# A state-space layer with an FP4 feed-forward block on one core: the transposes of x move behind those of h and into the layer's PSUM bank

## The chip, the cores and the metric

The kernel runs on one core of a Trainium2 chip. The metric is the device time of one launch in microseconds (us). A NeuronCore has five engines that run side by side, each with its own queue in program order: TensorE (PE in the profile; PEld is its weight load), VectorE (DVE), ScalarE (ACT), GpSimd (POOL) and SyncE (SP), which here issues the DMAs. They wait for one another through semaphores.

## The reference, cut to what matters

Only the first sizes differ from the helper code: x is 4 x 2048 x 256, the feed-forward width is 704, the state has 16 entries.

```python
def L0_attn(x, A, B, C, D, gamma, beta):
    xB = jnp.einsum('bsh,nh->bsn', x, B)
    xD = jnp.einsum('bsh,oh->bso', x, D)
    def step(state, xb_t):
        state = state @ A.T + xb_t
        return (state, state)
    _, states = jax.lax.scan(step, init, jnp.swapaxes(xB, 0, 1))
    out = jnp.einsum('bsn,hn->bsh', states, C) + xD
    return layernorm(out) * gamma + beta

def fp4_quant_dequant(x):                  # blocks of 16 along the last dim
    scale = max(max(abs(xb)) / 6.0, 1e-12)
    idx = jnp.searchsorted(_MID, jnp.abs(xb / scale))
    return _GRID[idx] * sign(xb) * scale

def L0_ffn(x, w_gate, w_up, w_down):       # each product quantises both operands
    gate = fp4_linear(x, w_gate)
    y = fp4_linear(x, w_up)
    return fp4_linear(jax.nn.silu(gate) * y, w_down)

x = layernorm(x + L0_attn(x, ...))
x = layernorm(x + L0_ffn(x, ...))
```

## The kernel before

A first phase of about 70 us loads x and the weights, quantises and transposes the weights and computes the chunk states of the scan. After it a pipeline runs over 64 tiles of 128 rows. Each tile passes through these operations:

- **layer** (PE, L1017 and the helper's L1006): C times the states plus D times x, into the PSUM bank `yb`, columns 0 to 255. Then `mean_square` (ACT L573), the reciprocal root on POOL (L457), `scale_gamma` (DVE L760, which works in `yb` itself) and `add_x` (DVE L767, the last reader of `yb`, semaphore `s_x1p`). ACT's `norm2` (L647) gives x1.
- Quantisation of x1: `x_max`, `x_scale` and `x_recip` on DVE, `x_norm` on POOL (L467), `x_abs` on ACT, `x_sum` (L788) and `x_grid` (L794) on DVE, and last `x_scale` on POOL (L472, semaphore `s_qx`).
- **x_turn** (PE L1027): two transposes of the quantised x1 into `xt`, which is part of the PSUM tensor `turned`. `x_hi` (ACT L610) copies them to `xtHi`, `x_lo` (DVE L799, semaphore `s_xlo`) computes the rest into `xtLo`.
- **gu0, gu1, gu2** (PE L1006): the gate and up products in three column cuts, six products each, into the three banks of `gu`. `silu_gate` (ACT L614) and `times_up` (DVE L806, which waits for the end of gu2) follow.
- Quantisation of h: `h_max`, `h_scale` and `h_recip` on DVE (L810, L815, L820), `h_norm` on POOL (L477), `h_abs` on ACT, `h_sum` (L825) and `h_grid` (L830) on DVE, `h_scale` on POOL (L482, semaphore `s_qh`).
- **h_turn** (PE L1059): six transposes into `ht`, which shares its bank of `turned` with `xt`. `h_hi` (ACT L627) and `h_lo` (DVE L835, `s_lo`) follow.
- **ffn_down** (PE L1006, 18 products into `db`), `add_x1` (DVE L842, `s_r`), and the last layernorm on ACT and POOL; SP stores the tile.

The order on each engine is written out by hand: a list of operations, each with a lag. In step s, an operation with lag k works on tile s - k. The lists are unrolled in program order, so each engine runs one tile of every operation in each step:

```python
run(pe, [(h_turn, 6), (gu1, 4), (gu2, 4), (x_turn, 3), (layer, 0), (ffn_down, 6), (gu0, 3)], ...)
run(pool, [(h_norm, 6), (x_scale, 4), (pow3, 10), (t_lo, 0), (add_beta, 0), (x_norm, 3), (pow2, 2),
           (h_scale, 6), (pow1, 1)])
run(dve, [(x_grid, 2), (scale_gamma, 0), (x_max, 1), (add_x, 0), (x_scale, 1), (h_lo, 5), (x_recip, 1),
          (h_sum, 4), (times_up, 3), (h_grid, 4), (x_lo, 2), (h_max, 3), (add_x1, 5), (h_scale, 3),
          (x_sum, 1), (h_recip, 3)], ...)
```

Below, n is the tile whose h PE turns in a step. In that step PE works on h_turn(n), gu1 and gu2(n+2), x_turn(n+3), layer(n+6), ffn_down(n) and gu0(n+3). From the lists follows what lies side by side on the others: DVE runs `h_lo(n)`, `h_sum(n+1)`, `times_up(n+2)`, `h_grid(n+1)`, `x_lo(n+3)`, `h_max(n+2)`, `add_x1(n)`; POOL runs `h_norm(n+1)` and right behind it `x_scale(n+3)`.

Of the kernel before, what the change touches and what calls it, by code (L numbers as in the profile page):

```python
# [48 lines left out]
def ssm_fp4_ffn(nc, x, A, B, C, D, gamma, beta, w_gate, w_up, w_down, out):  # L49
    BATCH, SEQ, H = x.shape  # L50
# [4 lines left out]
    TILES = HALVES * CHUNK  # L55
# [46 lines left out]
    with ExitStack() as ctx:  # L102
# [3 lines left out]
        def bank(name):  # L106
            return ctx.enter_context(nc.psum_tensor(name, [P, 512], F32))
# [84 lines left out]
        yb = bank("yb")  # L192
        turned = ctx.enter_context(nc.psum_tensor("turned", [P, 2 * 512], F32))
# [1 line left out]

        GU_CUTS = [(0, 512), (512, 1024), (1024, GU)]
        amH = gu[:, GU:GU + FB]
        xt = turned[:, 0:H]
        ht = turned[:, H:H + NKD * P]
        db = turned[:, 512:512 + H]  # L200
        hm = grid[:, 0:FF]
# [59 lines left out]
        def run(eng, ops, after={}):  # L261


            last = max(lag for _, lag in ops)

            def step(h, i, inside):
                for op, lag in ops:
                    if inside or 0 <= CHUNK * h + i - lag < TILES:
                        op(h, i - lag)

            for h in range(PEELED):
                for i in range(CHUNK):
                    step(h, i, False)
                    for extra in after.get(CHUNK * h + i, ()):
                        extra()
            with eng.Fori(PEELED, HALVES) as h:
                for i in range(CHUNK):
                    step(h, i, True)
            for i in range(last):
                step(HALVES, i, False)  # L280

        def done(h, m):

            return h * CHUNK + (m + 1)

        def done_dma(h, m):

            return h * (16 * CHUNK // RING) + 16 * (m // RING + 1)

        def w_target(g, low):  # L290

            _, what, k, n = W_GROUPS[g]
            src = wbanks[g % 3]
            if what == "gu":
                dst = (wguLo if low else wguHi)[:, :, k * P:(k + n) * P].rearrange("p c (r k) -> p r c k", k=P)
                return dst, src[:, 0:n * KH * P].rearrange("p (r c k) -> p r c k", r=n, c=KH)
            first = 0 if what == "dA" else KDA
            return ((wdLo if low else wdHi)[:, first:first + KDA, k * P:(k + 1) * P],
                    src[:, 0:KDA * P].rearrange("p (c k) -> p c k", k=P))
# [554 lines left out]
        def _(pe):  # L854
# [77 lines left out]
            def chunk_states(b, positions=range(CHUNK)):  # L932

                pe.wait_ge(s_gc, KH)
                pe.wait_ge(s_xtc, 4 * KH * (b + 1))
                for t in positions:
                    for c in range(KH):
                        ins = nc.tensor.matmul(fBank[b // BPP][:, b % BPP * CPB:(b % BPP + 1) * CPB],  # L938
                                               gPad[:, c, N * t:N * t + P], xT[:, t, c, b * CPB:(b + 1) * CPB],
                                               start=(b % BPP == 0 and t == 0 and c == 0),  # L940
                                               stop=(t == CHUNK - 1 and c == KH - 1), skip_group_check=True)
                if CHUNK - 1 in positions:
                    ins.then_inc(s_loc, 1)
# [58 lines left out]
            def split_products(to, terms, first=True):  # L1002

                passes = [(l, r) for (lh, ll), (rh, rl) in terms for l, r in ((lh, rh), (lh, rl), (ll, rh))]
                for q, (l, r) in enumerate(passes):
                    ins = nc.tensor.matmul(to, l, r, start=(first and q == 0), stop=(q == len(passes) - 1))  # L1006
                return ins

            def layer(h, m):

                r = m % RING
                tile = h * CHUNK + m
                pe.wait_ge(s_tlo, done(h, m))
                pe.wait_ge(s_ld[r], 3 * done_dma(h, m))
                if not isinstance(tile, int) or tile >= 1:
                    pe.wait_ge(s_x1p, done(h, m - 1))
                nc.tensor.matmul(yb[:, 0:H], stTile[:, r, :], cStack[:, :], start=True, stop=False)  # L1017
                split_products(yb[:, 0:H], [((tHi[:, m % 2, c, :], tLo[:, m % 2, c, :]), (dHi[:, c, :], dLo[:, c, :]))
                                            for c in range(KH)], first=False).then_inc(s_y, 1)

            def x_turn(h, m):
                tile = h * CHUNK + m
                pe.wait_ge(s_qx, done(h, m))
                if not isinstance(tile, int) or tile >= 3:
                    pe.wait_ge(s_lo, done(h, m - 3))
                for c in range(KH):
                    ins = nc.tensor.transpose(xt[:, c * P:(c + 1) * P], xm[:, m % 2, c * P:(c + 1) * P], ident[:, :])  # L1027
                ins.then_inc(s_tx, 1)

            def ffn_up(k):  # L1030
                first, last = GU_CUTS[k]

                def op(h, m):
                    tile = h * CHUNK + m
                    if k == 0:
                        pe.wait_ge(s_xlo, done(h, m))
                    if not isinstance(tile, int) or tile >= 1:
                        pe.wait_ge([s_silu, s_h, s_hsc][k], done(h, m - 1))
                    ins = split_products(gu[:, first:last],
                                         [((xtHi[:, m % 2, c, :], xtLo[:, m % 2, c, :]),  # L1040
                                           (wguHi[:, c, first:last], wguLo[:, c, first:last])) for c in range(KH)])
                    if k >= 1:
                        ins.then_inc([s_gate, s_up][k - 1], 1)
                return op

            def h_turn(h, m):
                tile = h * CHUNK + m
                pe.wait_ge(s_qh, done(h, m))
                if not isinstance(tile, int) or tile >= 1:
                    pe.wait_ge(s_lo, done(h, m - 1))  # L1050
                    pe.wait_ge(s_r, done(h, m - 1))
                else:
                    pe.wait_ge(s_states, PAIRS)
                if isinstance(tile, int) and tile + 2 >= TILES:
                    pe.wait_ge(s_xlo, TILES)
                else:
                    pe.wait_ge(s_xlo, done(h, m + 2))
                for q, row in enumerate(KD):
                    ins = nc.tensor.transpose(ht[:, q * P:(q + 1) * P], hq[:, m % 2, row:row + P], ident[:, :])  # L1059
                ins.then_inc(s_t, 1)  # L1060

            def ffn_down(h, m):
                tile = h * CHUNK + m
                pe.wait_ge(s_lo, done(h, m))
                if isinstance(tile, int) and tile == 0:
# [3 lines left out]

            chunk_states(BATCH - 1, FILL_STATES[-1])  # L1070
            gu0, gu1, gu2 = (ffn_up(k) for k in range(3))
            run(pe, [(h_turn, 6), (gu1, 4), (gu2, 4), (x_turn, 3), (layer, 0), (ffn_down, 6), (gu0, 3)],
                {step_: [*(lambda ts=ts: chunk_states(BATCH - 1, ts) for ts in (FILL_STATES.get(step_),) if ts),
                         *(lambda k=k: link(1, k) for k in FILL_CHAIN.get(step_, ()))] for step_ in range(CHUNK)})

# [27 lines left out]
```

## Time and profile before

| what | value |
|---|---|
| time, median of 3 runs | 636.41 us (634.6 to 637.58) |
| the profiled execution: time | 634.62 us |
| its span | 632.8 us |
| PE busy | 602.9 us (95%) |
| DVE, ACT, POOL busy | 514.5, 477.8, 465.6 us |
| TensorE clock granted, mean | 0.973 of full speed |

The span is the stretch from the first to the last recorded instruction; the time of a run holds 1.8 us more. The busy time of an engine is what its instructions cover. Matmuls overlap one another in the records, so the pace of PE is read from the distance of their starts rather than from their durations.

### The profile page before, as it was taken

The numbers are of one execution on the slowest core, as the hardware profiler recorded it, in microseconds if no ns is written. First come the engines' busy times: TensorE is split into PE (matmuls) and PEld (weight loads), VectorE is DVE, ScalarE is ACT, GpSimd is POOL, SyncE is SP. The second block draws the span as 40 slices with busy tenths as digits, with TensorE's granted clock in tenths as the row PEclk, the third lists the DMA queues.
The fourth block names the chain that finished last, engine by engine and source line by source line (L and its number), as shares of the span: only waits on it lengthen the run. The fifth ranks groups of instructions, "written<-read, shape, count | busy, mean of one in ns | idle before, by whom it ended". The sixth has DMA issues, their size and how long they took to land.

```text
span 632.8 us, 12672 instructions
## 1 busy us (share of the span) xinstructions
PE 602.9 (95%) x3705; PEld 525.8 (83%) x3705; DVE 514.5 (81%) x1226; ACT 477.8 (75%) x1422; POOL 465.6 (74%) x602
## 2 busy tenths in 40 slices
PE   5999968999999999999999999999999999999984
PEld 3787747788888888888888888888888888888874
DVE  2694126999999999999999999999999999999972
ACT  3455326778888888888888888888888888888764
POOL 1461316878888888888888888888888888887652
PEclk9999957999999999999999999999999999999996
DMA  6743111111111111111111111111111111110001
GB/s 247 260 138 101 46 30 50 42 38 46 53 54 54 53 47 54 52 46 53 53 53 53 53 53 53 52 50 48 53 52 52 53 52 45 53 34 9 25 18 41
DMA packets 46171, 38.32 MB, mean 61 GB/s; under 512 B 6912, under 2 KB 44864, under 8 KB 45120
## 3 DMA queue, kind: packets, MB, share of 16 engines
q1 hardware_dynamic: 46144, 37.99, 19.5%
q8 instruction: 13, 0.21, 0.1%
q14 instruction: 14, 0.11, 0.1%
HBM read 19.50 MB, written 8.39 MB: 44 GB/s over the span
## 4 chain that ended last, share of the span: by engine, by line
PE 90%; ACT 3%; DVE 2%; issue 1%; DMA 1%; POOL 1%; SPq 1%; POOLq 0%; DVEq 0%; ACTq 0%
PE gu L1006 39%; PE turned L1006 21%; PE yb L1006 9%; PE turned L1059 7%; PE yb L1017 3%; PE turned L1027 2%; PE gu L938 2%; PE yb L912 2%; PE gu L912 1%; DMA scratch<-in_L_attn_x_dram 1%; PE turned L938 1%; ACT xT L525 1%; PE turned L974 1%; SPq L377 1%; POOL scratch L482 0%
## 5 line engine op out<-in xcount | busy, mean ns | idle before, releaser
L1006 PE MATMUL gu<-wguHi,xtHi 128*128 128x512 f32 (+1 forms) x384 | 151.0, 393 | 1.3 <-DVE xtLo L799 1.3
L1006 PE MATMUL gu<-wguLo,xtHi 128*128 128x512 f32 (+1 forms) x384 | 145.6, 379 | 0.0
L1006 PE MATMUL gu<-wguHi,xtLo 128*128 128x512 f32 (+1 forms) x384 | 145.5, 379 | 0.0
L477 POOL TENSOR_TENSOR scratch<-scratch 128x704 f32<-128x704 f32 x64 | 92.3, 1442 | 57.5 <-DVE scratch L820 57.5
L1006 PE MATMUL turned<-wdHi,htHi 128*128 128x256 f32 x384 | 109.9, 286 | 3.8 <-DVE htLo L835 3.8
L1006 PE MATMUL turned<-wdLo,htHi 128*128 128x256 f32 x384 | 109.2, 284 | 0.0
L1006 PE MATMUL turned<-wdHi,htLo 128*128 128x256 f32 x384 | 108.4, 282 | 0.0
L482 POOL TENSOR_TENSOR scratch<-scratch 128x704 f32<-128x704 f32 x64 | 89.1, 1392 | 9.5 <-DVE scratch L830 9.4
L627 ACT CAST htHi<-turned 128x768 fp32r<-128x768 f32 x64 | 51.4, 804 | 57.9 <-PE turned L1059 57.9
L1006 PEld LDWEIGHTS gu<-wguHi,xtHi 128*128 128x128 f32 x384 | 73.0, 190 | 11.4 <-DVE xtLo L799 2.1
L1006 PEld LDWEIGHTS gu<-wguHi,xtLo 128*128 128x128 f32 x384 | 72.6, 189 | 11.7
L1006 PEld LDWEIGHTS gu<-wguLo,xtHi 128*128 128x128 f32 x384 | 72.8, 189 | 9.1
L1006 PEld LDWEIGHTS turned<-wdHi,htHi 128*128 128x128 f32 x384 | 72.6, 189 | 4.2 <-DVE htLo L835 4.2
L1006 PEld LDWEIGHTS turned<-wdHi,htLo 128*128 128x128 f32 x384 | 73.8, 192 | 0.0
L1006 PEld LDWEIGHTS turned<-wdLo,htHi 128*128 128x128 f32 x384 | 73.0, 190 | 0.0
L835 DVE TENSOR_TENSOR htLo<-turned,htHi 128x768 fp32r<-128x768 f32 x64 | 61.3, 958 | 13.3 <-ACT htHi L627 6.2
L842 DVE SCALAR_TENSOR_TENSOR scratch<-turned,scratch 128x256 f32<-128x256 f32 x64 | 27.2, 424 | 42.5 <-PE turned L1006 42.5
L462 POOL TENSOR_TENSOR tLo<-xtTile,tHi 128x256 fp32r<-128x256 f32 x64 | 47.4, 740 | 18.2 <-ACT tHi L606 18.2
L806 DVE TENSOR_TENSOR scratch<-scratch,gu 128x704 f32<-128x704 f32 x64 | 56.0, 875 | 2.3 <-PE gu L1006 2.3
L810 DVE TENSOR_REDUCE gu<-scratch 128x44 f32<-128x704 f32 x64 | 56.6, 884 | 0.0
L830 DVE SCALAR_TENSOR_TENSOR scratch<-grid,scratch 128x704 f32<-128x704 f32 x64 | 56.6, 884 | 0.0
L1059 PEld LDWEIGHTS turned<-ident,scratch 128*128 128x128 f32 x384 | 45.7, 140 | 10.9 <-POOL scratch L482 2.4
(169 smaller groups left out, 1593.4 us busy)
## 6 DMA issues: line engine op xcount, KB each, us to landing
scratch<-in_L_attn_x_dram SPq DMA_DIRECT2D x8, 1024.0 KB, 5.1
xtTile<-xT SPq DMA_DIRECT2D x64, 128.0 KB, 2.3
scratch<-in_L_attn_x_dram SPq DMA_DIRECT2D x64, 128.0 KB, 2.4
out_dram<-scratch SPq DMA_DIRECT2D x64, 128.0 KB, 1.9
stTile<-statesHi SPq DMA_DIRECT2D x128, 8.0 KB, 1.7
stTile<-statesLo SPq DMA_DIRECT2D x64, 8.0 KB, 1.7
scratch<-in_L_ffn_w_down_dram SPq DMA_DIRECT2D x1, 704.0 KB, 7.5
scratch<-in_L_ffn_w_up_dram SPq DMA_DIRECT2D x1, 640.0 KB, 6.0
```

Of the source, the lines that this page charges most:

```text
L462: nc.gpsimd.tensor_tensor(tLo[:, m % 2, :, :], xtTile[:, m % RING, :, :], as_f32(tHi[:, m % 2, :, :]), ALU.subtract).then_inc(s_tlo, 1)
L477: nc.gpsimd.tensor_tensor(blocks(hx[:, m % 2, :]), blocks(hx[:, m % 2, :]), each_block(hRc[:, m % 4, :], FB), ALU.mult).then_inc(s_xnh, 1)
L482: nc.gpsimd.tensor_tensor(blocks(hq[:, m % 2, :]), blocks(hq[:, m % 2, :]), each_block(hSc[:, m % 4, :], FB), ALU.mult).then_inc(s_qh, 1)
L627: nc.scalar.copy(htHi[:, m % 2, :, :].rearrange("p c k -> p (c k)"), ht).then_inc(s_hi, 1)
L806: nc.vector.tensor_tensor(hx[:, m % 2, :], silu[:, m % 2, :], gu[:, FF:GU], ALU.mult).then_inc(s_h, 1)
L810: nc.vector.tensor_reduce(amH, blocks(hx[:, m % 2, :]), AX_X, ALU.max, apply_absolute_value=True).then_inc(s_ham, 1)
L830: nc.vector.scalar_tensor_tensor(out=hq[:, m % 2, :], in0=hm, scalar=LEAST, in1=hx[:, m % 2, :], op0=ALU.max, op1=ALU.subtract, reverse1=T ...
L835: nc.vector.tensor_tensor(htLo[:, m % 2, :, :].rearrange("p c k -> p (c k)"), ht, as_f32(htHi[:, m % 2, :, :]).rearrange("p c k -> p (c k) ...
L842: nc.vector.scalar_tensor_tensor(out=x1[:, j, :], in0=db, scalar=1.0, in1=x1[:, j, :], op0=ALU.mult, op1=ALU.add, accum_out=sum3[:, j:j + ...
L912: ins = nc.tensor.transpose(to[:, q * P:(q + 1) * P], xRaw[:, h % 2, (t * KH + q) * P:(t * KH + q + 1) * P], ident[:, :])
L1006: ins = nc.tensor.matmul(to, l, r, start=(first and q == 0), stop=(q == len(passes) - 1))
L1059: ins = nc.tensor.transpose(ht[:, q * P:(q + 1) * P], hq[:, m % 2, row:row + P], ident[:, :])
```

## The change

`xt`, the target of x's two transposes, leaves the bank of `turned` that it shared with `ht` and becomes columns 256 to 511 of the layer's bank `yb`. In PE's list x_turn moves from behind gu2 to right behind h_turn. The waits are changed to fit: x_turn no longer waits for `h_lo` of three tiles back but for `add_x` of tile m+2 (`s_x1p`), which ends the use of `yb` by the layer's result; h_turn no longer waits for `x_lo`; and layer(m) now waits for `x_lo(m-3)`, the last reader of `xt`.

```diff
-        xt = turned[:, 0:H]
+        xt = yb[:, H:2 * H]
@@ layer
                     pe.wait_ge(s_x1p, done(h, m - 1))
+                if not isinstance(tile, int) or tile >= 3:
+                    pe.wait_ge(s_xlo, done(h, m - 3))
                 nc.tensor.matmul(yb[:, 0:H], stTile[:, r, :], cStack[:, :], start=True, stop=False)
@@ x_turn
                 pe.wait_ge(s_qx, done(h, m))
-                if not isinstance(tile, int) or tile >= 3:
-                    pe.wait_ge(s_lo, done(h, m - 3))
+                if isinstance(tile, int) and tile + 2 >= TILES:
+                    pe.wait_ge(s_x1p, TILES)
+                else:
+                    pe.wait_ge(s_x1p, done(h, m + 2))
@@ h_turn
-                if isinstance(tile, int) and tile + 2 >= TILES:
-                    pe.wait_ge(s_xlo, TILES)
-                else:
-                    pe.wait_ge(s_xlo, done(h, m + 2))
@@ the order on PE
-            run(pe, [(h_turn, 6), (gu1, 4), (gu2, 4), (x_turn, 3), (layer, 0), (ffn_down, 6), (gu0, 3)],
+            run(pe, [(h_turn, 6), (x_turn, 3), (gu1, 4), (gu2, 4), (layer, 0), (ffn_down, 6), (gu0, 3)],
```

On PE, at the head of a step (h_turn, L1059), before the change:

```order
 L1059 MATMUL turned<-ident,scratch 128x128 [waits s_r,s_xlo,s_lo,s_qh]
 L1059 MATMUL turned<-ident,scratch 128x128 x5
 L1006 MATMUL gu<-wguHi,xtHi 128x512 [waits s_h]
 L1006 MATMUL gu<-wguLo,xtHi 128x512
 L1006 MATMUL gu<-wguHi,xtLo 128x512
```

And in the changed kernel, the same place:

```order
 L1059 MATMUL turned<-ident,scratch 128x128 [waits s_r,s_lo,s_qh]
 L1059 MATMUL turned<-ident,scratch 128x128 x5
 L1031 MATMUL yb<-ident,scratch 128x128 [waits s_x1p,s_qx]
 L1031 MATMUL yb<-ident,scratch 128x128
 L1006 MATMUL gu<-wguHi,xtHi 128x512 [waits s_h]
 L1006 MATMUL gu<-wguLo,xtHi 128x512
```

The two transposes of x, with their wait for POOL's `s_qx`, now stand ahead of the twelve products of gu1 and gu2.

On PE, between the end of gu2 and ffn_down, before the change:

```order
 L1006 MATMUL gu<-wguHi,xtLo 128x384
 L1027 MATMUL turned<-ident,scratch 128x128 [waits s_lo,s_qx]
 L1027 MATMUL turned<-ident,scratch 128x128
 L1017 MATMUL yb<-cStack,stTile 128x256 [waits s_x1p,s_ld2,s_tlo]
 L1006 MATMUL yb<-dHi,tHi 128x256
```

And in the changed kernel:

```order
 L1006 MATMUL gu<-wguLo,xtHi 128x384
 L1006 MATMUL gu<-wguHi,xtLo 128x384
 L1019 MATMUL yb<-cStack,stTile 128x256 [waits s_x1p,s_xlo,s_ld2,s_tlo]
 L1006 MATMUL yb<-dHi,tHi 128x256
 L1006 MATMUL yb<-dLo,tHi 128x256
```

The layer now follows gu2 directly and has one more wait, for DVE's `s_xlo`. On DVE the order is the same before and after; around the instruction that signals `s_xlo` (L799) the changed kernel has:

```order
 L825 SCALAR_TENSOR_TENSOR scratch<-grid,scratch 128x704 [waits s_mh]
 L806 TENSOR_TENSOR scratch<-scratch,gu 128x704 [waits s_up,s_silu]
 L830 SCALAR_TENSOR_TENSOR scratch<-grid,scratch 128x704 [waits s_hsum]
 L799 TENSOR_TENSOR xtLo<-yb,xtHi 128x256 [waits s_xhi]
 L810 TENSOR_REDUCE gu<-scratch 128x44 [waits s_h]
```

Nothing moved there; what L799 reads is now `yb`. It stands behind `times_up` (L806), whose `s_up` is signalled by the last product of gu2.

## Rows read from the trace of the kernel before

**Rows 1.** The page, its first two parts: busy time, and PE and clock in 40 slices.
```profile
PE 602.9 (95%) x3705; PEld 525.8 (83%) x3705; DVE 514.5 (81%) x1226; ACT 477.8 (75%) x1422; POOL 465.6 (74%) x602
...
PE   5999968999999999999999999999999999999984
...
PEclk9999957999999999999999999999999999999996
```

**Rows 2.** Timeline of PE, one step: start us, duration, engine, line, operands, count.
```profile
301.86 0.82 PE L1059 MATMUL turned<-ident,scratch 128*128 128x128 f32 x6
...
302.43 0.48 PE L1006 MATMUL gu<-wguHi,xtHi 128*128 128x512 f32 x1
...
304.81 0.34 PE L1006 MATMUL gu<-wguHi,xtLo 128*128 128x384 f32 x1
...
304.98 0.38 PE L1027 MATMUL turned<-ident,scratch 128*128 128x128 f32 x2
...
305.29 0.38 PE L1017 MATMUL yb<-cStack,stTile 48*128 48x256 f32 x1
...
306.42 0.28 PE L1006 MATMUL turned<-wdHi,htHi 128*128 128x256 f32 x1
...
308.46 0.28 PE L1006 MATMUL turned<-wdHi,htLo 128*128 128x256 f32 x1
```

**Rows 3.** The same timeline, DVE and POOL, with idle time before and its releaser.
```profile
300.65 0.42 DVE L842 SCALAR_TENSOR_TENSOR scratch<-turned,scratch 128x256 f32<-128x256 f32 x1 [0.65 <-PE turned L1006]
...
301.45 0.42 DVE L820 RECIPROCAL scratch<-scratch 128x44 f32<-128x44 f32 x1
...
301.95 1.44 POOL L477 TENSOR_TENSOR scratch<-scratch 128x704 f32<-128x704 f32 x1 [0.95 <-DVE scratch L820]
...
303.36 0.62 POOL L472 TENSOR_TENSOR scratch<-scratch,xSc 128x256 f32<-128x256 f32 x1
...
305.33 0.88 DVE L806 TENSOR_TENSOR scratch<-scratch,gu 128x704 f32<-128x704 f32 x1
...
306.92 0.42 DVE L799 TENSOR_TENSOR xtLo<-turned,xtHi 128x256 fp32r<-128x256 f32 x1
...
308.78 0.43 DVE L842 SCALAR_TENSOR_TENSOR scratch<-turned,scratch 128x256 f32<-128x256 f32 x1 [0.65 <-PE turned L1006]
```

**Rows 4.** Timeline, late: x_turn ahead of ffn_down, and PE released by DVE.
```profile
603.59 0.38 PE L1027 MATMUL turned<-ident,scratch 128*128 128x128 f32 x2
603.72 0.36 PE L1006 MATMUL turned<-wdHi,htHi 128*128 128x256 f32 x1
...
615.91 0.96 DVE L835 TENSOR_TENSOR htLo<-turned,htHi 128x768 fp32r<-128x768 f32 x1 [1.55 <-ACT htHi L627]
...
616.93 0.39 PE L1006 MATMUL turned<-wdHi,htHi 128*128 128x256 f32 x1 [1.88 <-DVE htLo L835]
```

**Rows 5.** Timeline, early: DVE released by the end of gu2.
```profile
104.85 0.34 PE L1006 MATMUL gu<-wguHi,xtLo 128*128 128x384 f32 x1
...
105.29 0.89 DVE L806 TENSOR_TENSOR scratch<-scratch,gu 128x704 f32<-128x704 f32 x1 [2.27 <-PE gu L1006]
```

**Rows 6.** PE by stretches: us, PE busy (instructions), granted clock, DMA share, GB/s.
```profile
75.00:80.00 5.00, 4.08 (x26) 0.94 0.31 85
80.00:85.00 5.00, 2.90 (x16) 0.50 0.27 73
...
620.00:622.00 2.00, 0.87 (x6) 1.00 0.00 0
622.00:624.00 2.00, 1.13 (x5) 0.54 0.18 65
```

**Rows 7.** Timeline of PE at the low clock, and where it rose again.
```profile
97.43 0.58 PE L1017 MATMUL yb<-cStack,stTile 48*128 48x256 f32 x1
...
99.38 0.63 PE L1006 MATMUL gu<-wguHi,xtHi 128*128 128x512 f32 x1
...
103.51 0.40 PE L1006 MATMUL gu<-wguLo,xtHi 128*128 128x512 f32 x1
```

## The prediction, made before the changed kernel was run

> **What bounds the kernel now.** I read the page first: PE is busy 95% of the span, the others 74 to 81%, and PE's digits are 9 from the eighth slice to the third from the end, at full clock [rows 1]. The next view is the timeline of one step. Two `add_x1` (DVE L842) stand at 300.65 and 308.78 us, so a step lasts 8.13 us [rows 3]; the first slices and the last ones are start and end, and between them one step repeats. PE's rows of that step show no gap: h_turn at 301.86, gu1 at 302.43, the end of gu2 at 304.81 + 0.34 = 305.15, x_turn at 304.98, the layer at 305.29, ffn_down from 306.42 to 308.46 + 0.28 = 308.74 [rows 2]. DVE waits 0.65 us for ffn_down in every step and POOL 0.95 us for DVE's `h_recip` [rows 3]. So PE sets the pace and the other engines follow it with about a microsecond in hand.
>
> With so full an engine the question for a moved instruction is not what it costs, but whether its operands are there at the new place. The new order puts two waits on PE that the trace lets one date.
>
> **The first wait: x_turn on POOL.** In this step x_turn(n+3) needs POOL's `x_scale(n+3)` (L472), which ends at 303.36 + 0.62 = 303.98 [rows 3]. At its old place, 304.98, that was done a microsecond before. At the new place PE arrives at 302.43 [rows 2], 1.6 us too early. POOL cannot be earlier: x_scale stands right behind `h_norm(n+1)` (L477, from 301.95), which waits for `h_recip(n+1)` (DVE L820, 301.45 + 0.42), which stands behind `add_x1(n-1)` (300.65), which waits for the end of the previous step's ffn_down [rows 3]. So this is no fixed delay that slides away once the engines are shifted; it ties x_turn to PE's own previous ffn_down. Behind the waiting x_turn everything of PE is queued: gu1, gu2, the layer, ffn_down. The other new wait there, `add_x(n+5)`, ends earlier in the same DVE pass than `h_lo`, well before POOL is done, and costs nothing.
>
> **The second wait: the layer on x_lo.** layer(n+6) now waits for `x_lo(n+3)` of the same step. DVE runs it behind `times_up(n+2)` and `h_grid(n+1)`, and times_up waits for the end of gu2(n+2), which PE has only just finished. From the start of times_up at 305.33 to the end of x_lo at 306.92 + 0.42 = 307.34 are 2.01 us [rows 3]. Before, the layer started at 305.29, two microseconds ahead of that end [rows 2]; nothing asked it to wait. This wait follows gu2 wherever gu2 is, so it comes on top of the first. Behind it are queued the layer, ffn_down, gu0 and h_turn.
>
> **The ring and its length.** Both waits lie on one closed ring, which I add up from the end of one ffn_down to the end of the next:
> - ffn_down ends 308.74, add_x1 starts 308.78, 0.04 later; from add_x1 to the start of h_norm 301.95 - 300.65 = 1.30 [rows 2, 3]. Sum 1.34.
> - h_norm start to x_scale end: 303.98 - 301.95 = 2.03 [rows 3].
> - PE takes up work after a wait 616.93 - 616.87 = 0.06 later [rows 4].
> - x_turn takes 603.72 - 603.59 = 0.13 where nothing holds the next product [rows 4]; gu1 start to gu2 end 305.15 - 302.43 = 2.72 [rows 2]. Sum 2.85.
> - gu2 end to times_up: 105.29 - 105.19 = 0.10 where DVE waited for it [rows 5].
> - times_up start to x_lo end 2.01, and 0.06 until PE starts [rows 3, 4].
> - layer start to the end of ffn_down 308.74 - 305.29 = 3.45 [rows 2].
>
> The sum is 1.34 + 2.03 + 0.06 + 2.85 + 0.10 + 2.01 + 0.06 + 3.45 = 11.90 us against 8.13, so 3.77 us more for each step. What the step holds beside (gu0, h_turn, h_hi, h_lo, silu, the layernorms, the loads) runs in the gaps of this ring: h_turn is over 302.43 - 300.61 = 1.8 us after the end of the previous ffn_down (308.74 - 8.13 = 300.61), and x_turn starts 3.4 us after it. The work taken away saves nothing here: the wait ahead of the old layer (0.31 from x_turn to the layer instead of 0.13) lay on PE, but the ring contains a fresh wait in its place.
>
> **How many steps.** ffn_down runs for tiles 0 to 57 while the layer still runs, which makes 57 whole rings: 57 x 3.77 = 214.9 us. In steps 3 to 6, the start, ffn_down does not close the ring; the layer's wait costs at least 0.10 + 2.01 + 0.06 = 2.17 and at most 3.77 each. I take 2.4, near the lower end, since h_norm does not yet hold POOL in the first of them: 9.6. In the last three steps with an x_turn there is no layer, and only the first wait is paid, at most 304.04 - 302.43 = 1.61 each; I take 4 for the three. Together 228.5. The profiled execution has a span of 632.8, so 861.3, and with the 1.8 us that lie outside the span 863.1. The median of the runs is 1.8 above the profiled time, so **865** if the clock holds. Errors of 0.1 us a ring would make 6 us.
>
> **The clock.** PE then works 8 of 12 us, with gaps of 1.6 and 2.2 us in each ring. The trace shows the granted clock fall from full to half speed (2.4 to 1.2 GHz) in two places. Between 75 and 80 PE was busy 4.08 of 5 us, with small products, and the clock was 0.50 from 80 on; around 622 it fell behind a stretch with 0.87 busy of 2 us [rows 6]. At the low level the layer took 99.38 - 97.43 = 1.95 us instead of 1.13, and the products were back at 0.40 us each from 103.51, about 6 us after PE had begun to work without a gap [rows 7]. In the ring the stretch without a gap (layer, ffn_down, gu0) lasts 4.8 us at full clock. So a fall in a gap costs between nothing (clock holds) and half of 6 us = 3.0 for each ring. The ring resembles the two places where it fell in that PE waits again and again for an answer from another engine; its runs between the waits are denser than there. I take the middle of the two prices, 1.5 us a ring: 61 x 1.5 = 91.5, and 865 + 91.5 = **956**.
>
> The Trainium skill (TensorE: Matmul & The Clock Gate, section "Why this matters for your kernels") ties a drop in the middle of a kernel to idle gaps longer than either of the two here; by it the clock holds and the time is the 865. The trace does not quite agree with that: at 75 to 80 us the clock fell though PE was idle for less than 1 of 5 us [rows 6].
>
> **The rivals.**
> - *The clock holds* (865). For it: in the tail, at 620 to 622, it was still full with PE busy under half of the time [rows 6]. Against it: the fall right behind that.
> - *It stays low for the whole dense run, or falls in both gaps* (956 to 865 + 61 x 3.0 = 1048). For it: the rise took 6 us in the start.
> - *Only the first wait counts*, because x_lo is done before the layer gets there. Then the ring is 1.34 + 2.03 + 0.06 + 0.13 + (304.98 - 302.43) + 3.45 = 9.56, 1.43 more; 57 x 1.43 and some 10 for the ends give 728. Against it: DVE's order puts x_lo behind times_up without exception.
> - *Only the second wait counts*: 61 x 2.17 = 132, 769. It would need POOL's x_scale to run ahead of h_norm; its list says otherwise.
> - *Faster*: the transposes stand together, and the layer is no longer held behind its own: 0.31 - 0.13 = 0.18 for each of 61 steps, 11 us, 625. It decides at one point: `x_scale(n+3)` would have to end before 302.43, and it ends at 303.98; and x_lo before 305.15, and it ends at 307.34. Both are behind work that needs PE's previous result.
>
> **How the numbers follow.** Clock falls once a ring 0.58 (its own range 925 to 1005), clock holds 0.26, longer low stretches beyond 1005 0.08, one wait alone 0.05, faster 0.02, within the noise 0.01. The predicted time is that of the likeliest case, 956. The range reaches from 855, to take in the case of a held clock with its error, to 1005; outside are the upper end of the clock's price and the single waits. A measurement of this kernel can tell about 0.5% from no change, and nearly all cases are slower by far more.
>
> **What would show it.** In the profile after: the distance of two add_x1 11.9 us with a full clock, up to 13.5 with a fall; PE idle ahead of x_turn by 1.6 us, put down to POOL L472, some 60 times; PE idle ahead of the layer by 2.2 us, put down to DVE L799 (xtLo), 61 times; DVE's times_up waiting for gu2, which it hardly did before; PE's clock row with digits of 6 to 9 instead of 9. If PE has no gap ahead of the layer, my reading of the lags is wrong; if the distance is 11.9 and the clock row still reads 9, the sum was right and the clock's term was not.

## The result, and the profile after

| | before | after |
|---|---|---|
| time, median | 635.62 us (4 runs) | 948.47 us (4 runs, 946.23 to 950.09) |
| ratio | | 1.491 (95% interval 1.487 to 1.495) |
| span of the profiled execution | 632.8 us | 948.3 us |
| PE busy | 602.9 us (95%) | 698.6 us (74%) |
| mean granted clock of TensorE | 0.973 | 0.877 |

The changed kernel takes half as long again. The forecast was 956, in a range of 855 to 1005. The page of the changed kernel, the lines that answer to [rows 1]:

```profile
PE 698.6 (74%) x3705; PEld 601.0 (63%) x3705; DVE 520.3 (55%) x1226; ACT 475.6 (50%) x1422; POOL 469.4 (49%) x602
...
PE   6997677767776686767777677766777677767785
...
PEclk8987888898988989888898988989889898888996
```

DVE, ACT and POOL have the same work as before and less of the span; PE has the same 3705 matmuls, but 96 us more of busy time, and in the repeating part its clock row reads 8 and 9 by turns where it read 9 before. The view of the waits (who waited for whom, total us, times, longest us) names both new waits, the one for x_lo 61 times and the one for POOL 62 times:

```profile
DVE scratch L842 <- PE turned L1006: 244.6, 60, 4.3
...
PE yb L1019 <- DVE xtLo L799: 136.5, 61, 2.3
...
PE yb L1031 <- POOL scratch L472: 82.9, 62, 2.4
```

The first line is the mirror image: DVE, which waited 0.65 us a step for ffn_down [rows 3], now waits 2.8 or 4.3 us, because everything of PE comes later. One step of the timeline, in order of time (it answers to [rows 2, 3]; L1019 is the layer's first product, L1031 x_turn, both shifted by the new lines):

```profile
501.08 0.89 DVE L806 TENSOR_TENSOR scratch<-scratch,gu 128x704 f32<-128x704 f32 x1 [1.61 <-PE gu L1006]
...
502.69 0.41 DVE L799 TENSOR_TENSOR xtLo<-yb,xtHi 128x256 fp32r<-128x256 f32 x1
...
503.25 0.35 PE L1019 MATMUL yb<-cStack,stTile 48*128 48x256 f32 x1 [2.27 <-DVE xtLo L799]
...
503.53 0.52 PE L1006 MATMUL yb<-dHi,tHi 128*128 128x256 f32 x1
...
504.92 0.41 PE L1006 MATMUL turned<-wdHi,htHi 128*128 128x256 f32 x1
...
507.05 0.28 PE L1006 MATMUL turned<-wdLo,htHi 128*128 128x256 f32 x1
...
508.19 0.42 DVE L842 SCALAR_TENSOR_TENSOR scratch<-turned,scratch 128x256 f32<-128x256 f32 x1 [4.29 <-PE turned L1006]
...
509.40 0.82 PE L1059 MATMUL turned<-ident,scratch 128*128 128x128 f32 x6
...
509.49 1.44 POOL L477 TENSOR_TENSOR scratch<-scratch 128x704 f32<-128x704 f32 x1 [2.75 <-DVE scratch L820]
...
510.89 0.62 POOL L472 TENSOR_TENSOR scratch<-scratch,xSc 128x256 f32<-128x256 f32 x1
...
511.56 0.44 PE L1031 MATMUL yb<-ident,scratch 128*128 128x128 f32 x2 [1.35 <-POOL scratch L472]
...
514.55 0.89 DVE L806 TENSOR_TENSOR scratch<-scratch,gu 128x704 f32<-128x704 f32 x1 [1.61 <-PE gu L1006]
```

Read from top to bottom this is the ring of the prediction: the end of gu2 releases times_up, x_lo follows behind h_grid, x_lo releases the layer, ffn_down's end releases add_x1, then h_recip, h_norm, x_scale, and x_scale releases x_turn. From one times_up to the next are 13.47 us. The layer's products in this step take 504.92 - 503.25 = 1.67 us instead of the 1.13 of [rows 2], and those of ffn_down are recorded at 0.41 us each instead of 0.28, until 0.28 returns at 507.05: the clock is at its lower level there. The windows view of PE around this step (columns: length, busy, clock, DMA share, GB/s):

```profile
500.00:503.00 3.00, 0.97 (x6) 1.00 0.00 0
503.00:507.00 4.00, 3.75 (x17) 0.58 0.00 0
507.00:511.00 4.00, 3.22 (x22) 1.00 0.23 71
```

The clock falls just behind the gap ahead of the layer, not in it, and is full again before ffn_down ends. In the repeating part its record turns to one half 0.1 to 1.8 us behind the start of the layer, a little later from one fall to the next, and after the latest ones comes a step without a fall. Of the 57 distances between the add_x1 of tiles 0 to 57, six are 11.98 to 12.00 us and 51 are 13.15 to 13.53, most of them 13.48: a step without and a step with a fall. Their mean is 13.29.

### The profile page after: what moved, and what is told of

It is laid out like the page before. It is cut to its first block, busy times and chain, and to the rows that moved or that the text cites. A ratio compares the mean times of both kernels' runs of the same rounds, so it can differ in the third digit from the quotient of the medians.

```text
span 948.3 us, 12661 instructions
## 1 busy us (share of the span) xinstructions
PE 698.6 (74%) x3705; PEld 601.0 (63%) x3705; DVE 520.3 (55%) x1226; ACT 475.6 (50%) x1422; POOL 469.4 (49%) x602
## 4 chain that ended last, share of the span: by engine, by line
PE 54%; DVE 21%; issue 12%; POOL 9%; ACT 2%; DMA 1%; SPq 0%; POOLq 0%; DVEq 0%; ACTq 0%
PE turned L1006 19%; PE gu L1006 17%; PE yb L1006 7%; DVE scratch L806 6%; DVE scratch L830 5%; POOL scratch L472 4%; POOL scratch L477 4%; PE yb L1031 3%; DVE scratch L842 2%; PE yb L1019 2%; DVE xtLo L799 2%; DVE scratch L820 2%; DVE scratch L788 2%; PE gu L938 2%; PE yb L912 1%
## 5 line engine op out<-in xcount | busy, mean ns | idle before, releaser
L1006 PE MATMUL turned<-wdHi,htHi 128*128 128x256 f32 x384 | 141.1, 367 | 3.8 <-DVE htLo L835 3.8
L1006 PE MATMUL turned<-wdLo,htHi 128*128 128x256 f32 x384 | 140.1, 365 | 0.0
L1006 PE MATMUL turned<-wdHi,htLo 128*128 128x256 f32 x384 | 139.2, 362 | 0.0
L1019 PE MATMUL yb<-cStack,stTile 48*128 48x256 f32 x64 | 23.2, 362 | 140.1 <-DVE xtLo L799 136.5
L1019 PEld LDWEIGHTS yb<-cStack,stTile 48*128 48x128 f32 x64 | 11.9, 187 | 158.5 <-issue 158.5
L806 DVE TENSOR_TENSOR scratch<-scratch,gu 128x704 f32<-128x704 f32 x64 | 56.8, 888 | 100.7 <-PE gu L1006 100.7
L1006 PEld LDWEIGHTS turned<-wdHi,htHi 128*128 128x128 f32 x384 | 107.3, 279 | 4.3 <-DVE htLo L835 4.3
L1006 PEld LDWEIGHTS turned<-wdLo,htHi 128*128 128x128 f32 x384 | 107.0, 279 | 0.0
L1006 PEld LDWEIGHTS turned<-wdHi,htLo 128*128 128x128 f32 x384 | 106.2, 277 | 0.0
L614 ACT ACTIVATE scratch<-gu 128x704 f32<-128x704 f32 x64 | 48.6, 760 | 105.0 <-PE gu L1006 105.0
L1031 PE MATMUL yb<-ident,scratch 128*128 128x128 f32 x128 | 28.2, 302 | 87.4 <-POOL scratch L472 82.9
L457 POOL TENSOR_TENSOR rs<-ve1t,neg_half 128x1 f32<-128x1 f32 x64 | 35.4, 553 | 98.3 <-ACT ve1t L580 98.3
L457 POOL TENSOR_TENSOR rs<-ve2t,neg_half 128x1 f32<-128x1 f32 x64 | 35.2, 549 | 96.0 <-ACT ve2t L580 96.0
```

Source lines behind the costliest of these rows:

```text
L457: nc.gpsimd.tensor_tensor(dst[:, j:j + 1], src[:, j:j + 1], neg_half[:, :], ALU.pow).then_inc(signal, 1)
L614: nc.scalar.activation(silu[:, m % 2, :], gu[:, 0:FF], ACT.Silu).then_inc(s_silu, 1)
L806: nc.vector.tensor_tensor(hx[:, m % 2, :], silu[:, m % 2, :], gu[:, FF:GU], ALU.mult).then_inc(s_h, 1)
```

## The experiments

The theory has three terms: the wait of x_turn for POOL, the wait of the layer for x_lo, and a fall of the clock in the gap that the second one leaves. The first four kernels take one of them away each (in e3 a wait for h_lo stands in for the one for POOL).

**e1, work added.** If the clock's term is real, giving PE something to do in the gap must make the kernel faster. Edit, in `layer`, ahead of its waits for add_x and x_lo:

```diff
+                if not isinstance(tile, int) or tile >= 6:
+                    pe.wait_ge(s_lo, done(h, m - 6))
+                    for _ in range(12):
+                        nc.tensor.matmul(db, wdHi[:, 0, 0:P], wdHi[:, 1, :], start=True, stop=True)
```

> The changed kernel plus twelve extra products of 256 columns on PE between gu2 and the layer's new wait, from constant weights into the bank that ffn_down overwrites; they wait for h_lo of the tile, as ffn_down does. They add about 12 x 0.12 = 1.4 us of work a step and lie wholly in the 2.2 us gap ahead of the layer. Theory (the ring of two waits sets 11.9 us a step, and a fall of the clock in that gap adds 1.6): the ring is as long as before, the clock does not fall, the step is 11.9 us and the time about 863, some 85 us below the changed kernel although PE does more. Rival 1 (the step of 13.5 is the ring's own length, the clock is a by-product): the fillers change nothing, 948. Rival 2 (PE's own work is what counts): 1.4 us a step more, about 1035.

Measured 874.51 us, 1.375 of before (1.370 to 1.380), 74 us less than the changed kernel. With 58 x 12 products more the kernel is faster. Its clock row and the step's rows (timeline; L1018 is the filler, L1023 the layer):

```profile
PEclk9999589999999999999999999999999999999998
```

```profile
502.22 1.60 PE L1018 MATMUL turned<-wdHi 128*128 128x256 f32 x12
...
502.49 0.89 DVE L806 TENSOR_TENSOR scratch<-scratch,gu 128x704 f32<-128x704 f32 x1 [1.62 <-PE gu L1006]
...
504.09 0.41 DVE L799 TENSOR_TENSOR xtLo<-yb,xtHi 128x256 fp32r<-128x256 f32 x1
...
504.65 0.36 PE L1023 MATMUL yb<-cStack,stTile 48*128 48x256 f32 x1 [0.84 <-DVE xtLo L799]
```

The fillers lie in the wait and shorten PE's idle time from 2.27 to 0.84 us, the clock stays full between the start and the end, and all 57 steps read 11.98 to 12.04 us. The six steps without a fall in the changed kernel read the same. So the ring is 11.99 us long and the clock cost 13.29 - 11.99 = 1.30 us a step on the mean, 1.49 in a step with a fall. The time is 11.5 us above the expected 863; where they lie is said below, under the ends. Rival 1 (948) and rival 2 (1035) fall.

**e2, the bank alone.** The changed kernel with `run(pe, ...)` in the old order, x_turn behind gu2.

> The changed kernel with PE's old order: x_turn stands behind gu2 again, its target stays in the layer's bank with both new waits. Theory: the first wait (POOL's x_scale) goes, the second (layer on x_lo) stays, since DVE's x_lo is behind times_up either way: 8.13 + 2.0 = 10.2 us a step with a full clock, 757 us, and up to 1.6 us a step more (855) where the clock falls in that gap; I expect something between, near 800. Rival (the move on PE is what costs, the bank is harmless): near 636.

Measured 780.6 us (one run). Its steps are 10.28 us, with a pair of about 11.4 and 12.1 every nine or ten steps where the clock fell, ten steps of the 57 in all, 10.55 on the mean. The wait for POOL is gone and the one for x_lo stands as before:

```profile
PE yb L1019 <- DVE xtLo L799: 127.8, 61, 2.7
```

The bank's wait costs 10.28 - 8.13 = 2.15 us a step with x_turn at its old, harmless place. The rival (near 636) falls.

**e3, the order alone.** The kernel before with x_turn moved in PE's list and nothing else, so that x's target stays in `turned`.

> The kernel before with only PE's order changed: x_turn directly behind h_turn, its target still in h's bank, so that it waits for h_lo of the h just turned instead of add_x, and the layer has no new wait. Theory: x_turn waits both for x_scale (3.4 us after ffn_down's end) and for h_lo (about 3.9 us after it), the wait ahead of the layer is absent: 3.95 + 2.68 + 3.45 = 10.1 us a step with a full clock, 745 us, up to 1.6 us a step more (835) where the clock falls in the gap of 2.1 us. Rival (x_turn's place is harmless, only the bank's wait costs): near 636.

Measured 773.65 us (one run), steps of 10.26 us. PE waits for h_lo here, as the old bank demands, and not ahead of the layer:

```profile
504.35 0.41 PE L1027 MATMUL turned<-ident,scratch 128*128 128x128 f32 x2 [1.97 <-DVE htLo L835]
```

The move alone costs 2.13 us a step, nearly what the bank alone costs, and no step of the repeating part has a fall. The bank change was the way to avoid this wait for h_lo, but POOL's x_scale is nearly as late: it ends at 503.67 here, 0.53 us before h_lo. The wait for POOL itself is not measured by this kernel but by the next one.

**e4, x_lo early.** The changed kernel with `x_lo` ahead of `times_up` on DVE and `x_hi` ahead of `silu_gate` on ACT.

> The changed kernel with x_lo moved ahead of times_up on DVE and x_hi ahead of silu_gate on ACT, nothing else. Theory: x_lo is then done about 5.2 us after ffn_down's end, before gu2 ends at 6.3, so the layer's wait is free and only the first wait is left: 9.56 us a step, and since the gap of 1.6 us ahead of x_turn did not bring the clock down in the changed kernel, a full clock: about 725 us. Rival (each of the waits alone already costs the most of it, or the clock falls in the first gap as well): 1.6 us a step more, 815.

Measured 736.51 us (one run), steps of 9.67 us. The layer follows gu2 without a wait, x_turn waits 1.36 us for POOL, and the clock holds; two rows of the timeline and one of the windows (PE, PEld, DVE, ACT, POOL busy, clock):

```profile
500.72 0.44 PE L1031 MATMUL yb<-ident,scratch 128*128 128x128 f32 x2 [1.36 <-POOL scratch L472]
...
503.26 0.33 PE L1006 MATMUL gu<-wguHi,xtLo 128*128 128x384 f32 x1
...
503.53 0.38 PE L1019 MATMUL yb<-cStack,stTile 48*128 48x256 f32 x1
```

```profile
400.00:500.00 100.00, 85.82 (x528) 73.31 (x526) 77.09 (x191) 73.42 (x218) 72.02 (x93) 1.00 0.16 44
```

Two moved entries, one in each list, take back 212 of the 313 us. The second wait is worth 11.99 - 9.67 = 2.32 us of ring and with it the whole of the clock's term; the first is worth 9.67 - 8.13 = 1.54.

**e5, x_scale early.** The changed kernel with `x_scale` ahead of `h_norm` in POOL's list.

> The changed kernel with x_scale ahead of h_norm in POOL's list, nothing else. Theory: x_turn then waits only for x_grid and x_scale (2.3 us after ffn_down's end instead of 3.4), so the first wait shrinks from 1.6 to 0.5 us a step; the layer's wait and the clock's fall in it stay. With a full clock 11.99 - 1.13 = 10.9 us a step and about 808 us; with one fall a step 12.4 and about 895. Since the gap ahead of the layer is the same 2.2 us, I expect most steps with a fall: 880. Rival (the first wait is hidden behind the second): 948, no gain.

Measured 871.23 us (one run), near the expected 880, but not for the expected steps. Without a fall they read 11.29 us, 0.70 less than 11.99, where I had expected 1.13 less; with a fall 12.4 to 12.8, and only 29 of the 57 steps have one, though PE idles the same 2.3 us ahead of the layer. Why fewer, no run shows. The timeline shows what became late in place of POOL:

```profile
425.75 0.62 POOL L472 TENSOR_TENSOR scratch<-scratch,xSc 128x256 f32<-128x256 f32 x1 [3.37 <-DVE scratch L794]
426.30 0.41 DVE L767 SCALAR_TENSOR_TENSOR scratch<-yb,scratch 128x256 f32<-128x256 f32 x1
...
426.64 1.10 DVE L778 TENSOR_SCALAR xSc<-xAm 128x16 f32<-128x16 f32 x1
...
426.87 0.41 PE L1031 MATMUL yb<-ident,scratch 128*128 128x128 f32 x2 [0.38 <-DVE scratch L767]
```

x_scale ends at 426.37, but x_turn starts at 426.87, released by add_x (L767, to 426.71): the third of the new waits, which I had rightly priced at nothing in the prediction and then forgotten when POOL no longer covered it. The rows show one thing more: L778 takes 1.10 us where it takes 0.30 in the changed kernel. It stands behind add_x and does not hold up x_turn, but e8 meets it again.

**e6, all early.** PE's order and bank as changed, and every operand made earlier (of DVE's list only the new one is shown):

```diff
-run(pool, [(h_norm, 6), (x_scale, 4), (pow3, 10), ...
+run(pool, [(x_scale, 4), (h_norm, 6), (pow3, 10), ...
-(h_hi, 7), (h_abs, 6), (silu_gate, 5), (nm2, 2), (x_hi, 4), ...
+(h_hi, 7), (x_hi, 4), (h_abs, 6), (silu_gate, 5), (nm2, 2), ...
+run(dve, [(scale_gamma, 0), (add_x, 0), (x_max, 1), (x_scale, 1), (h_lo, 5), (x_lo, 2), (x_recip, 1),
+          (h_sum, 4), (times_up, 3), (h_grid, 4), (h_max, 3), (x_sum, 1), (x_grid, 1), (add_x1, 5),
+          (h_scale, 3), (h_recip, 3)], ...
```

> The changed kernel's order and bank on PE, with both operands made in time: x_sum and x_grid before add_x1 and add_x before x_max on DVE, x_lo right behind h_lo, x_hi behind h_hi on ACT, x_scale ahead of h_norm on POOL. Theory: both waits and the falls of the clock vanish and PE sets the pace again. The four runs before show that two transposes cost PE the same at either place (0.19 us ahead of gu1; 0.48 - 0.27 = 0.21 between gu2 and the layer), so the step is 8.1 us and the time that of the kernel before, 636, within 0.5%. Rival 1 (the move itself would have been a gain, 0.18 us a step as the kernel before has it between x_turn and the layer): 625. Rival 2 (a part of the cost is neither wait, for example the transposes in the layer's bank): a step above 8.3 and more than 645.

Measured 682.76 us, 1.074 of before (1.071 to 1.077). Both priced waits and the falls are gone, yet a step takes 8.79 us, not 8.13: rival 2. In the timeline:

```profile
407.19 1.39 POOL L482 TENSOR_TENSOR scratch<-scratch 128x704 f32<-128x704 f32 x1 [0.41 <-DVE scratch L830]
...
407.82 1.04 DVE L788 SCALAR_TENSOR_TENSOR scratch<-scratch 128x256 f32<-128x256 f32 x1
...
408.89 0.42 DVE L794 SCALAR_TENSOR_TENSOR scratch<-scratch 128x256 f32<-128x256 f32 x1
```

x_sum (L788), at the median 0.42 us in all kernels so far, takes 1.04 where it starts beside POOL's h_scale, and ends 0.28 us after it (408.86 against 408.58). That makes add_x1 late, then add_x, and x_turn waits for add_x (`PE yb L1031 <- DVE scratch L767: 39.4, 62, 4.8` in the view of the waits). How much of the 0.66 us of the step is owed to the long x_sum no run isolates; e8 took it away, but met another long instruction.

**e7, x_sum alone.** To measure that by itself: the kernel before with `x_sum` moved ahead of `add_x1`.

> The kernel before with x_sum (DVE L788) moved ahead of add_x1 on DVE, nothing else. In the last experiment L788 took 1.04 us there instead of 0.42. Theory (it and POOL's h_scale cannot run at once: L788 starts while POOL L482 still has 0.6 us to go, waits for its end and then takes its 0.42): here too L788 reads about 0.95 us, add_x1 starts some 0.25 us later, and the step stays 8.13 since h_turn needs add_x1 only 0.5 us later: 636. Rival (L788 was long there for another reason, such as x_abs of the other schedule or the layer's bank): L788 stays 0.42 us.

Measured 639.32 us (one run), steps of 8.13 us. L788 reads:

```profile
L788 DVE SCALAR_TENSOR_TENSOR scratch<-scratch x64: 424/864/866, 95.7 to 601.5; 128x256 f32<-128x256 f32 x64
```

(shortest, median and longest in ns). Nothing else was changed, so the longer time belongs to the place beside h_scale, which runs here from 406.04 to 407.43; L788, from 406.85, ends at 407.71, again 0.28 us after it. The 0.65 us for which DVE idles ahead of add_x1 in the kernel before absorbed it: add_x1 starts at 407.63, 0.08 us after ffn_down's end, where it was 0.04. The 3 us over the kernel before's 636.29 lie in the last six steps, 45.4 us instead of 42.0.

**e8, x_sum away from POOL's operations.** e6 with `x_sum` and `x_grid` behind `add_x1` and `h_scale`, and `h_recip` behind `add_x` in the next pass.

> The all-early kernel with x_sum and x_grid behind add_x1 and h_scale on DVE, where POOL is idle, and h_recip moved behind add_x to the head of the next pass. Theory (what e6 lost was L788's 0.6 us, which made add_x1 late by 0.5 and with it add_x, on which x_turn waits): L788 is back at 0.42, add_x ends 2.1 us after ffn_down instead of 2.4, x_turn waits about 0.35 us, a step is 8.5 us and the time about 660. The wait for add_x cannot go to zero, as scale_gamma and add_x stand behind add_x1 on DVE. Rival (the rest of e6's loss is neither of the waits): 682 again.

Measured 688.46 us, 1.082 of before (1.077 to 1.087); 660 was expected. L788 is back at 0.42 us and PE waits 0.42 us for add_x, where about 0.35 was worked out. But another instruction stands beside POOL's work now, and with x_lo behind it the layer waits again (0.17 us):

```profile
408.05 1.39 POOL L477 TENSOR_TENSOR scratch<-scratch 128x704 f32<-128x704 f32 x1 [0.66 <-DVE scratch L820]
...
408.28 1.19 DVE L778 TENSOR_SCALAR xSc<-xAm 128x16 f32<-128x16 f32 x1
```

L778 took 0.30 us at 303.12 in the kernel before; here it takes 1.19 and ends at 409.47, 0.03 us behind POOL's h_norm (409.44). The 0.30 was no undisturbed length either: 303.42 is 0.03 us behind the end of h_norm too. The step is 8.92 us. That x_turn at the new place could be had for free was not shown: two orders were tried on the other engines, neither as fast as the kernel before.

## Why the prediction was right, point by point

**The first wait** held as to place and releaser. PE idles 1.35 us ahead of x_turn for POOL L472, where the prediction had 1.6. The two count from different points: the 1.6 from the place where the next instruction starts when nothing holds it, 302.43 - 301.86 = 0.57 us behind the start of h_turn [rows 2], the 1.35 from the end of h_turn's record, 0.82 behind it. Counted as in the prediction it is 511.56 - 509.40 - 0.57 = 1.59. e4 isolates it: 1.54 us a step against the 1.43 of the rival "only the first wait counts" (728 us; measured 736.51).

**The second wait** held as well: 2.27 us ahead of the layer, 61 times. e2 isolates it at 2.15 us a step against 2.17; taken out of the changed ring, in e4, it is 2.32.

**That they add up** along one ring was the core of the sum: 11.90 predicted, 11.99 in e1. The two measured apart, 1.54 and 2.15, make 3.69 of the 3.86 us. Two terms were small by 0.06 and 0.09: x_turn to gu1 takes 511.75 - 511.56 = 0.19 rather than 0.13, and the layer starts 503.25 - 503.10 = 0.15 after x_lo ends rather than 0.06. The two rows in [rows 4] from which I took them have ffn_down behind the transposes and behind DVE's signal, not gu1 or the layer; the products of the sum should have been looked at in their own kind. What makes the 0.15 no run shows: x_turn, too, started 0.15 behind DVE in e3, and 0.05 behind POOL in e4. The other terms agree within 0.03.

**The clock** was the term in doubt, and I took 1.5 us between 0 and 3.0. It is 1.49 in a step with a fall and 1.30 on the mean of the 57. That the size came out so well is luck: I had no row that gave it, only the middle of two bounds, and the upper bound took the 6 us from the start [rows 7]. In the step shown above the slow products reach from 503.53 to 507.05, 3.5 us, in which they stand 0.21 us apart instead of 0.12, and that makes the 1.5. That the clock fell behind the second gap and never behind the first was not in the prediction.

**The ends.** add_x1 of tile 0 comes at 136.12 instead of 121.87, 14.3 us later, where 9.6 and four times the clock's 1.5 made 15.6. That they agree is partly luck: 2.2 of the 14.3 stand ahead of the first layer (73.49 instead of 71.25), where nothing was changed and where the kernels here lie between 69.2 and 73.5, and the clock fell in two of the four steps only. The 57 steps gave 57 x (13.29 - 8.13) = 294, where 215 + 86 = 301 stood. Behind them come 6.9 us more, against 4: the last three steps with an x_turn are 1.7, 1.9 and 2.0 us longer, and not at most 1.61. Together 315.5, the difference of the spans. e1, expected at 863 and profiled at 875.4, has 14.5 at the start against 9.6, 57 x 0.09 = 5 more in the steps, and 6.1 at the end against 4, together 12.

**The rule on idle gaps** in the Trainium skill (TensorE: Matmul & The Clock Gate, "Why this matters for your kernels"), by which the clock would have held and the time been 865, did not hold here: with gaps of 2.3 us that come back every 13 us it fell in 51 of 57 steps.

**Faster by standing together** was priced at 0.18 us a step. e4 shows that there is no such gain: from the last product of gu2 to the layer are 503.53 - 503.26 = 0.27 us without transposes, against 305.29 - 304.81 = 0.48 with them [rows 2], so they cost 0.21 at the old place and 0.19 at the new one.

## What to carry to other kernels

When an instruction is moved up on an engine that is never idle, look up when its operand is finished, then follow that operand's queue back: if it stands behind work that needs the moving engine's own previous result, the wait is part of a ring and is paid in every step, and two such waits on one ring add up. A shared bank turns the last reader of one half into a condition for the writer of the other; here a read of 0.4 us stood behind 1.6 us of other work in DVE's queue, and moving it up, with its bank as changed, gave back 212 of the 313 us. An idle gap on TensorE may have a second price in the clock; a few useless products in it tell in one run whether it has.

## What the runs showed of the hardware

- Similar gaps did not cost the clock alike. Ahead of the layer 2.27 us of idle time were followed by a fall in 51 of the 57 steps of the changed kernel and in 29 of 57 in e5, 2.1 us at the same place in e2 in ten of 57, 1.97 us behind the transposes of h in e3 and 1.36 us in e4 in none of the repeating part. I have no rule for it; all that is shown is that filling the gap of the changed kernel kept the clock up.
- DVE and POOL can hold each other up. x_sum (L788), whose two inputs lie in SBUF, took 0.42 us with POOL idle, 0.86 and 1.04 beside POOL's h_scale, and ended 0.28 us behind it. L778, one small input, ended 0.03 us behind h_norm in nearly every step of every kernel, and took 0.30, 1.10 or 1.19 us by how long h_norm still had to go; in e6, at 252.48, where h_norm was not running, it took 0.17. The other way round, POOL's L457 took 0.73 us beside the long x_sum in e6 and e7, and 0.55 in all the others. L810 and L773, reductions, and L825 and L830, with one input in PSUM, were not stretched beside POOL's work (0.88, 0.41, 0.83 and 0.88 us). The Trainium skill (SBUF — State Buffer, "SBUF: two separate sides") describes a port pair that DVE and GpSimd take in turn, each for a whole instruction, which DVE needs for two SBUF inputs or a fast mode. The durations agree with that in the main; that x_sum and L778 ended sooner behind POOL than their own 0.42 and 0.17 us it does not explain, and that L778 ran in such a mode no run here shows.
